# A GNN layer with a mixture-of-experts feed-forward: an expert chunk is spread over two trips of the main loop

## What is computed

```python
edge_index = jnp.stack([src, dst])
x = x + _L0_gnn_ref(_layernorm(x), edge_index, gnn_weight, gnn_bias)
x = x + _L0_ffn_ref(_layernorm(x)[None], gate_w, gate_b, w1, b1, w2, b2)[0]

def _L0_gnn_ref(x, edge_index, weight, bias):      # src, dst = edge_index
    agg = segment_sum(x[src], dst) / maximum(deg, 1)
    out = concatenate([x, agg], -1) @ weight        # 512 -> 256
    return out / norm(out) + bias

def _L0_ffn_ref(h, gate_w, gate_b, w1, b1, w2, b2): # 8 experts, 256 -> 1024 -> 256
    probs = softmax(x @ gate_w + gate_b); idx = argmax(probs); prb = max(probs)
    pos = rank of the token among those of its expert; kept = pos < C   # C = 977
    hmid = relu(buf @ w1 + b1);  ybuf = hmid @ w2 + b2
    y = ybuf[idx, min(pos, C - 1)] * (prb * kept)
```

## Time and profile before

| | |
|---|---|
| median of 3 runs | 1421.02 us (1415.76 to 1421.2) |
| the profiled execution | 1421.57 us, span 1419.8 us |
| mean granted TensorE clock | 0.968 of full |
| busy in the span | TensorE 1175.7 us, weight load 899.7, VectorE 862.1, ScalarE 474.8, GpSimd 877.3 |
| main loop | about 60 to 1240 us, of which trips with a chunk from about 256 us |
| DMA | 130 GB/s on the mean, 184 MB |

### The profile page before, as it was taken

How to read it: one execution, slowest core, us unless ns; L and a number is a source line. 1 busy time by engine, 2 the same in 40 slices (tenths; PEclk the granted TensorE clock), 3 DMA queues, 4 the chain that set the end, 5 groups by cost and what they waited for, 6 DMA issues and landing times.

```text
span 1419.8 us, 30155 instructions
## 1 busy us (share of the span) xinstructions
PE 1175.7 (83%) x5349; PEld 899.7 (63%) x5350; DVE 862.1 (61%) x3753; ACT 474.8 (33%) x1384; POOL 877.3 (62%) x933
## 2 busy tenths in 40 slices
PE   1076676889898989899989898989899999877885
PEld 0065565677777777777777777777767676654553
DVE  7645454666666666666666666666666666654443
ACT  3411112233333333333333333333333333343342
POOL 3167667777777777777777777777777777511101
PEclk9989888999999999999999999999999999988998
DMA  8686868443444443434343434343434443311111
GB/s 248 203 262 193 262 208 253 127 135 116 138 118 137 117 138 111 138 111 131 107 130 105 130 105 129 105 131 107 126 108 126 112 120 111 99 31 37 44 43 36
DMA packets 114562, 184.19 MB, mean 130 GB/s; under 512 B 21611, under 2 KB 85408, under 8 KB 114544
## 3 DMA queue, kind: packets, MB, share of 16 engines
q0 software_dynamic: 43424, 109.52, 27.9%
q1 hardware_dynamic: 71120, 74.48, 17.2%
HBM read 156.08 MB, written 36.09 MB: 135 GB/s over the span
## 4 chain that ended last, share of the span: by engine, by line
PE 45%; DVE 20%; DVEq 14%; issue 13%; DMA 6%; ACT 2%; SPq 1%; ACTq 0%; POOLq 0%; POOL 0%
PE ps_q L686 20%; PE ps_h L751 11%; PE ps_a L742 7%; DVE sel L994 5%; DVEq L1245 3%; PE ps_t L759 2%; DMA b_b<-in_L_ffn_b 2%; DVEq L851 2%; DMA ring<-xn_d,idx 2%; DMA out<-ys,node_i 2%; DVE row L1108 1%; DVE row L1112 1%; DVE bn L1114 1%; PE ps_b L770 1%; PE ps_q L691 1%
## 5 line engine op out<-in xcount | busy, mean ns | idle before, releaser
L458 POOL DMA_INDIRECT ring<-xn_d,idx x784 | 753.1, 961 | 305.3 <-issue 226.6
L686 PE MATMUL ps_q<-ring,sel 128*128 128x257 f32 (+1 forms) x1952 | 591.3, 406 | 121.2 <-DVE sel L994 88.5
L686 PEld LDWEIGHTS ps_q<-ring,sel 128*128 128x128 f32 x1952 | 342.2, 195 | 235.1 <-issue 172.3
L994 DVE SCALAR_TENSOR_TENSOR sel<-lane,block,dst_t 128x512 f32<-128x512 bf16 x245 | 184.1, 752 | 118.3 <-issue 82.3
L770 PE MATMUL ps_b<-w_sb,hid_t 128*128 x864 | 220.8, 386 | 12.6 <-ACT hid_t L605 8.1
L751 PE MATMUL ps_h<-w_sb,hid_t 128*128 x432 | 208.7, 610 | 5.6 <-ACT hid_t L584 5.6
L1003 DVE TENSOR_TENSOR acc<-acc,ps_q 128x257 f32 x245 | 103.3, 422 | 166.2 <-issue 128.2
L770 PEld LDWEIGHTS ps_b<-w_sb,hid_t 128*128 128x128 f32 x864 | 160.0, 190 | 38.4 <-issue 18.9
L472 POOL DMA_INDIRECT disp_d<-row,slot x53 | 54.7, 1031 | 124.0 <-DVEq L1065 120.3
L605 ACT ACTIVATE hid_t<-ps_t,b_t 128x128 f32<-128x128 f32 x432 | 117.2, 382 | 26.3 <-PE ps_t L759 26.3
L599 ACT ACTIVATE hid<-ps_h 128x512 f32<-128x512 f32 x108 | 64.5, 597 | 184.1 <-PE ps_h L751 184.1
(11 more groups left out here) (188 smaller groups left out, 1213.9 us busy)
## 6 DMA issues: line engine op xcount, KB each, us to landing
w_sb<-in_L_ffn_w SPq DMA_DIRECT2D x32, 512.0 KB
ring<-xn_d,idx POOLq DMA_INDIRECT x784, 2.8
disp_d<-hid SPq DMA_DIRECT2D x8, 1040.0 KB, 8.0
xs<-disp_d SPq DMA_DIRECT2D x55, 130.0 KB, 2.9
ys<-disp_d SPq DMA_DIRECT2D x55, 130.0 KB
b_b<-in_L_ffn_b SPq DMA_DIRECT2D x55, 128.0 KB
xb<-in_x SPq DMA_DIRECT2D x51, 128.0 KB
out<-row SPq DMA_DIRECT2D x51, 128.0 KB
```

The costliest lines, as they stand in the source:

```text
L458: pool.indirect_dma_start(ring[:, (k % 2) * TQ + j, 0:D], None, xn_d[:, :], bass.IndirectOffsetOnAxis(ap=idx[:, k * TQ + j:k * TQ + j + 1] ...
L686: mm = pe.matmul(ps[:, 0:width], sel[:, s, j, :], ring[:, (k % 2) * TQ + j, 0:width], start=(j == 0), stop=(j == TQ - 1), skip_group_check ...
L994: dve.scalar_tensor_tensor(out=sel[:, s, :, :], in0=lane[:, :].rearrange("p (j m) -> p j m", j=1).to_broadcast((P, TQ, P)), scalar=block0[ ...
```

## The change

A chunk now takes two trips. Of a pair, the first does `xc_transposes` and `up`, the second `hid_transposes` and `down`. So the main loop has 9 plain trips (0 to 8) and 20 pairs, and does 20 chunks in place of 41. The chunk's number `u` and the trip's number `t` are now apart (`SHIFT` is 21). `choose` may also take the last, partly filled chunk of an expert whose count has reached the cap of 977.

On VectorE, `choose` no longer runs woven into `route`, and `result` no longer into `finish_row`: each stands alone, behind a branch on the inner loop's count, `choose` in the second trip of a pair and `result` in the first. `finish_row` comes ahead of `result`. The row to be dispatched is copied to a tile of its own, `sent`, so that `new_row` no longer waits for the dispatch. On GpSimd, the dispatch of a trip stands behind the first four gathers of the next. On TensorE, the one-column product at the end of each visit (L691, fp32) goes: the fourth product now takes all 257 columns, and a one-column bf16 product carries the semaphore. In the late trips on TensorE, `counts` comes ahead of the expert work. In the first eight trips, SyncE sends the filler rows of `disp_d` for the next trip only when the dispatch of this one is through.

```diff
+PLAIN = C0 + 1
+PAIRS = (TRIPS - PLAIN) // 2
+SHIFT = TRIPS - (C0 + PAIRS)
...
+            fill_block(0)
+            with sp.Fori(0, C0 - 1) as t:
+                trip(t, weights=True)
+                sp.wait_ge(disp_out, 16 * (t + 1))
+                sp.sem_inc(sp_turn, 1)
+                fill_block(t + 1)
...
+            def trip(t, u=None, more=True, fill=False):
+                for k in range(1, QS):
+                    quad(t, k)
+                if more:
+                    quad(t + 1, 0)
+                scatters(t, u, fill=fill)
...
-                    width = AW if j < TQ - 1 else D
-                    mm = pe.matmul(ps[:, 0:width], sel[:, s, j, :], ring[:, (k % 2) * TQ + j, 0:width],
+                    mm = pe.matmul(ps[:, 0:AW], sel[:, s, j, :], ring[:, (k % 2) * TQ + j, 0:AW],
...
-                        mm = pe.matmul(ps[:, D:AW], sel[:, s, j, :], ring[:, (k % 2) * TQ + j, D:AW],
-                                       start=False, stop=True, skip_group_check=True)
+                        if final:
+                            mm = pe.matmul(ps[:, AW + 1:AW + 2], ones[:, :], ones[:, 0:1], start=True, stop=True,
+                                           skip_group_check=True)
...
                         [steps((node, linear, 0)),
                          steps((node, linear, 1)),
-                         steps((chunk, up, 0)),
+                         steps((first, up, 0), (second, hid_transposes, 0)),
+                         steps((second, hid_transposes, 1))],
+                        [steps((prev, counts), (quads, load_quads)),
+                         steps((first, up, 1), (second, down, (0, 1))),
+                         steps((second, down, (2, 3))),
                          steps()],
-                        [steps((prev, counts), (chunk, up, 1), (quads, load_quads)),
-                         steps((chunk, hid_transposes, 0)),
-                         steps((chunk, hid_transposes, 1)),
-                         steps((chunk, down, (0, 1)))],
-                        [steps((chunk, down, (2, 3))),
-                         steps((chunk, down, (4, 5))),
-                         steps((chunk, down, (6, 7))),
+                        [steps((second, down, (4, 5))),
+                         steps((second, down, (6, 7))),
+                         steps(),
                          steps((node, xl_transposes), (quads, turn_quads))]]
...
-                dve.wait_ge(disp_out, 16 * (t + 1))
...
+            def send_copy(t):
+
+                def copy():
+                    if not isinstance(t, int):
+                        dve.wait_ge(disp_out, 16 * t)
+                    dve.tensor_copy(sent[:, :], row[:, :])
+
+                return [nothing, copy]
...
+            def main_trip(t, half=None, u=None):
+                dve.load(next_regs, qtab[0:1, ds(t * QS + QS, QS), :])
+                dve.wait_ge(cat_ready, t + 1)
+                add_last(t, 0)
+                select_quad(t, 1)
+                chains(route(t), send_copy(t))
+                if half is not None:
+                    with dve.If(half > 0):
+                        dve.drain()
+                        chains(choose(u))
+                add_last(t, 1)
+                select_quad(t, 2)
+                chains(finish_row(t))
+                if half is not None:
+                    with dve.If(half < 1):
+                        chains(result(t, u, True))
+                add_last(t, 2)
+                select_quad(t, 3)
...
+            with dve.Fori(0, PLAIN) as t:
+                main_trip(t)
+            with dve.Fori(0, PAIRS) as i:
+                with dve.Fori(0, 2) as half:
+                    main_trip(dve.snap(i * 2 + half + PLAIN), half, dve.snap(i + C0))
```

More of the change, by code:

```diff
@@ L482, in results, with quad, scatters @@
                     bounds_check=N - 1, oob_is_err=False).then_inc(res_out, 16)
-            def trip(t, quads=True, prev=True, chunk=True, rows=P):
-                for k in range(QS):
-                    for j in range(TQ):
-                        if quads:
-                            gather(t, k, j)
-                if prev:
-                    dispatch(t, rows, fill=not chunk)
-                if chunk:
-                    results(t)
-            with pool.Fori(0, C0) as t:
-                trip(t, chunk=False)
-            with pool.Fori(C0, TRIPS) as t:
-                trip(t)
+            def quad(t, k):
+                for j in range(TQ):
+                    gather(t, k, j)
+            def scatters(t, u=None, prev=True, rows=P, fill=False):
+                if prev:
+                    dispatch(t, rows, fill)
+                if u is not None:
+                    results(u)
+            def trip(t, u=None, more=True, fill=False):
[4 more added lines that the diff above has]
+                scatters(t, u, fill=fill)
+            quad(0, 0)
+            with pool.Fori(0, C0) as t:
+                trip(t, fill=True)
+            trip(C0)
+            with pool.Fori(0, PAIRS - 1) as i:
+                t = pool.snap(i * 2 + PLAIN)
+                trip(t, i + C0)
+                trip(t + 1)
+            trip(TRIPS - 2, C0 + PAIRS - 1)
+            trip(TRIPS - 1, more=False)
             pool.load([last], ends[0:1, 0:1])
@@ L611, in trip @@
[L611 to L618 removed]
+                chunk_rows(c)
+                e = load_expert(u)
+                act.wait_ge(xc_ps, c)
+                act.activation(xc_t, ps_t[:, 0:KD, :], ACT.Copy).then_inc(xct_ready, 1)
@@ L708, in quad, with trip @@
                 pe.reg_add(n, n, 1)
-            def trip(t, quads=True, node=True, prev=True, chunk=True, rows=P):
-                c = chunks(t)
-                expert = []
+            expert = []
+            def trip(t, u=None, part=None, quads=True, node=True, prev=True, rows=P):
+                chunk = u is not None
+                c = chunks(u) if chunk else None
+                first, second = chunk and part == 0, chunk and part == 1
+                if not second:
+                    expert.clear()
                 def load_expert():
-                    pe.load(code, ctab[0:1, ds(t, 1), :])
+                    pe.load(code, ctab[0:1, ds(u, 1), :])
                     expert.append(pe.snap(code[1], min_val=0, max_val=EX - 1))
@@ L1161, in route, with choose, top_up @@
                 return [s0, s1, s2, s3, s4, s5, s6, s7, s8]
-            def choose(t, whole=True):
-                lim, least = (float((CAP // P) * P), float(P)) if whole else (float(CAP), 1.0)
-                have, cand, hit, take = (g8[0:1, r, :] for r in (4, 5, 4, 7))
+            def choose(u, whole=True):
+                least = float(P) if whole else 1.0
+                have, cand, hit, take, full = (g8[0:1, r, :] for r in (4, 5, 4, 7, 7))
                 def s0():
-                    dve.scalar_tensor_tensor(out=have, in0=seen[0:1, :], scalar=lim, in1=taken[:, :],
+                    dve.scalar_tensor_tensor(out=have, in0=seen[0:1, :], scalar=float(CAP), in1=taken[:, :],
                                              op0=ALU.min, op1=ALU.subtract)
+                    if whole:
+                        dve.tensor_scalar(full, seen[0:1, :], float(CAP), float(P - 1), ALU.is_ge, ALU.mult)
+                def top_up():
+                    dve.tensor_tensor(have, have, full, ALU.add)
                 def s1():
@@ L1241, in result @@
                 return [s0, s1, s2, s3, s4, s5, s6, s7]
-            def trip(t, quads=True, node=True, prev=True, chunk=True, next_node=True, next_known=None):
-                if quads:
-                    dve.load(next_regs, qtab[0:1, ds(t * QS + QS, QS), :])
-                    dve.wait_ge(cat_ready, t + 1)
-                    add_last(t, 0)
-                    select_quad(t, 1)
-                chains(route(t) if prev else [], choose(t, whole=prev) if chunk else [])
-                if quads:
-                    add_last(t, 1)
-                    select_quad(t, 2)
-                chains(result(t, node) if chunk else [],
-                       ([nothing] if chunk else []) + finish_row(t) if prev else [])
-                if quads:
-                    add_last(t, 2)
-                    select_quad(t, 3)
-                    for now, then in zip(regs, next_regs):
-                        dve.reg_mov(now, then)
+            def main_trip(t, half=None, u=None):
[16 more added lines that the diff above has]
+                select_quad(t, 3)
+                for now, then in zip(regs, next_regs):
+                    dve.reg_mov(now, then)
+                new_row(t)
+                add_last(t, 3)
+                normalise_row(t)
+                select_quad(t + 1, 0)
+                prepare_node(t + 1)
```

291 lines of the change are left out of this document (158 added, 133 removed).

## The result

The changed kernel takes **1508.16 us** (median of 4 runs, 1502.9 to 1510.93) against 1421.11 of the kernel before on the same chip: ratio **1.0615, 95% interval 1.0574 to 1.0656**. It is slower, 87 us by the medians. The profiled execution has a span of 1505.4 us, against 1419.8.

A forecast was written before the change was run, and what follows sets the result against it. VectorE's in-order chain was taken as the bound. From 1421.6 us: tail -20.2, late trips -5.4, longer pairs +87, trip 8 -2, copy +2, giving 1483 us; own range 1450 to 1515, overall range 1400 to 1540.

The forecast's parts named there:

- What bounds the kernel: Main loop: VectorE's in-order chain sets the pace, 23.88 us a period, though TensorE is busy 83%.
- The pair: Two-trip pairs in the main loop: 25.7 and 26.4 us, 26.05 a trip in place of 23.88, +87 us over 40.
- Count waits: VectorE's idle ahead of the counts' read (L1144): some 1.6 us in first trips, 1 us in second.
- second visit's wait: VectorE's idle before the second-visit select of the fourth quad in second trips: near 3 us.
- TensorE's load: TensorE's register load directly behind the counts in second trips, nothing queued ahead of it: taken as 2.0 us.
- The clock: TensorE at half speed in pairs: 0 in the sum, up to 61 us (1544); rival 1515 to 1550, chance 0.13.
- Tail and late trips: Behind the main loop: chunk-only trips from 9 to 7, -20.2 us; new_row not waiting in three late trips, -5.4.
- Smaller terms: Trip 8 becoming plain, -2 us; the copy in the first eight trips, +2; one-column product and GpSimd's order, nothing.
- The waits are covered: Rival: in pairs only VectorE's own 46.9 us counts, 23.45 a trip, 1379 us in all; chance 0.14.
- GpSimd is the bound: Rival: GpSimd sets the main loop's pace, 22.0 us a trip, 1320 us in all; chance 0.05.
- Instruction fetches: Rival: branches cost each main-loop trip another 2.58 us, +103, 1586 us in all; chance 0.04.

The follow-up runs named there:

- b_unweave2: Kernel before, with route then choose and result then finish_row unwoven in its chunk trips: 1527.22 us, ratio 1.0732.
- b_tail2: Kernel before, with only the new choose rule (an expert at its cap may give its last, partly filled chunk): 1416.63 us, ratio 0.9949.
- d_best: a_weave_load with VectorE's register load moved from the start of the trip to just ahead of finish_row: 1350.11 us, ratio 0.9518 to the kernel before.
- a_weave_load: Changed kernel with weaving put back inside the branches and TensorE's register load moved behind up and down: 1415.51 us, ratio 0.9973 to the kernel before.
- a_load: Changed kernel with TensorE's register load moved from behind the counts to behind the products of up and down: 1473.87 us.

## Why the prediction was right, and where it was off

The forecast was 1483 us by a longer VectorE chain with the load exposed; measured 1508. The mechanism stood, and the experiments bear it out by undoing its parts (-62, -34, together -93). The size is too small by 25 us, most of it in one term that the sum put at nothing: TensorE's clock.

- **What bounds the kernel.** VectorE's in-order chain, not TensorE at 83%: shown by b_unweave2, which lengthens only that chain and adds 105 us, and by b_tail2, where a longer choose costs 17. Part of the 105 is TensorE's low clock in the trips of 27.1 us.
- **The pair.** First trip 25.7 forecast, 25.63 measured; second 26.4, and 26.53 in the seven that kept the full clock in the third quad. Count waits 1.6 and 1 us, measured 1.69 and 1.01; second visit's wait near 3, measured 2.80; choose 2.45, measured 968.17 to 970.65, 2.48; the copy 0.25, measured 0.30. TensorE's load was put at 2.0 us and took 1.46; VectorE's has 2.80 and 3.13 of idle where it had 2.58, which made up for it by luck. That VectorE's idle is the load and not `cat_ready` or a product shows in d_best, where it falls to 1.47 and ends with ScalarE's `cat`. The Trainium skill ("Runtime: NRT & Kernel Launch", Instruction fetch mechanics) gives about 0.2 us a register, for registers loaded from HBM, an estimate of 1.6 us for eight; TensorE's 1.46, loaded from `qtab` in SBUF, is near it, VectorE's 2.80 and 3.13 are not. With these two periods in all trips from 9 to 47, and trip 8 at its 22.96, the loop would be 84.6 us longer, as forecast (40 trips of 2.17, less 2).
- **The clock** is the term that was mis-sized. The sum had 0, with a bound of 61. The loop is 108.8 us longer, not 84.6. Of the other 24 us, 20 are the ten second trips of 28.2 to 29.2, in which the third quad is at the lower level; four first trips of over 26 us add 6, and one short second trip takes 2 off. That the clock is the cause of the 20 rests on the rows of these trips; no run changed the clock alone. The Trainium skill ("TensorE: Matmul & The Clock Gate", HAM oscillation) says that idle gaps make the bursts behind them start cold. The trace agrees in part: behind 3.06 us of idle a pair of matmuls takes 1.22 us, but behind 3.5 us sixteen of them take 6.74 us in one trip and 3.75 in the next. The sum by that rule, 1544, was 36 too high, since nearly half of the second trips kept the full level where it mattered, and what is slow ahead of a wait costs nothing.
- **Tail and late trips.** -25.6 forecast, -28.1 measured by VectorE's mark. GpSimd scatters nine results from 1419.83 to 1501.99, some 10.2 us apart: the last late trip's, seven of chunk-only trips as forecast, and the one behind the loop.
- **Smaller terms.** 5.0 us ahead of trip 8 by VectorE's mark, where I had +2 for the copy; what the other 3 are I did not follow up. Trip 8 lost 1.0 us in place of 2.
- **Rivals.** "The waits are covered" would have given 1379 and asked for waits under 2.1 us a pair. They are 5.5 (1.69, 1.01 and 2.80), and even in a_weave_load 4.2 (1.08, 1.02 and 2.09), so no run tests what a pair without them takes. "GpSimd is the bound" falls: its gathers wait 481 us, before 305. Instruction fetches: the page has 17 packets on the instruction queue, before 14, so the loop isn't fetched again.
- **Left open.** Why second trips go round in threes of 28.7, 28.2 and 26.5 (a_load nearly ends it), and how much of d_best's gain the kernel before would get from the same move of the load: it wasn't tried.

## What to carry to other kernels

A busy share of 83% did not make TensorE the bound; two kinds of trip of the same length with different work on it told so beforehand. When a loop's kinds of work are split over trips, weave each kind anew inside its branch: here the dependent chains of tiny operations that had hidden each other, and the waits for other engines, were the larger part of the loss (62 us of 93). Put loads of registers where the engine that issues them waits anyway.

## What was not expected of the hardware

- An eight-register load with nothing queued ahead of it on VectorE stops it for 2.6 to 3.1 us; moved behind a 0.75 us operation, 1.56 is left in first trips, and in second trips it lies with the wait for the counts (1.71 together). The profile puts the idle down to "issue" or to a product on TensorE, never to the load.
- Filling TensorE's gaps raised its mean clock by 0.03 and made the kernel 13 us slower.
- Two tiny operations of 0.15 us each, one of them a dependent step of its own, made the trip 0.4 us longer (b_tail2).
- Behind gaps of the same 3.5 us, TensorE came back at the lower level in one trip and at the full level in the next.
